# A two-layer graph convolution on one core: in the second layer VectorE evicts the last of a batch's four halves, ScalarE the other three

## The reference

```
def gcn_conv(x, W, b, src, dst, n):
    h = x @ W
    deg = jnp.zeros((n,), h.dtype).at[dst].add(1.0) + 1.0
    dinv = jax.lax.rsqrt(deg)
    norm = dinv[src] * dinv[dst]
    agg = jax.ops.segment_sum(h[src] * norm[:, None], dst, num_segments=n)
    return agg + h * (dinv * dinv)[:, None] + b
h = gcn_conv(emb, W1, b1, src, dst, NTOKEN)     # 64 -> 128 features
nodes = gcn_conv(h, W2, b2, src, dst, NTOKEN)   # 128 -> 64 features
return nodes[input.reshape(-1)].reshape(b_, l_, NINP)
```

## Time and profile before

| | |
|---|---|
| median of 3 runs | 2735.33 us (2734.2 to 2742.24) |
| the profiled execution's own time | 2734.99 us |
| its span in the profile | 2733.2 us |
| second layer, all batches | about 1835 to 2648 us of the span |
| what comes after it (POOL's last DMAs) | about 2648 to 2733 us |
| busy over the span | PE 76%, PEld 63%, DVE 84%, ACT 71%, POOL 34% |

### The profile page before, as it was taken

One profiled execution on the slowest core, in us unless ns is written; L12 is line 12 of the kernel. 1 busy time (PEld: TensorE's weight loads), 2 busy tenths in 40 slices (PEclk: granted clock), 3 DMA queues, 4 the chain that ended last, 5 costly groups with the idle time before them and its releaser, 6 DMA issues.

```text
span 2733.2 us, 87732 instructions
## 1 busy us (share of the span) xinstructions
PE 2070.1 (76%) x36895; PEld 1733.2 (63%) x36895; DVE 2299.6 (84%) x3705; ACT 1928.9 (71%) x5267; POOL 931.5 (34%) x704
## 2 busy tenths in 40 slices
PE   3455555554453599899799999968999999999970
PEld 2344444444321467777678877857888888888860
DVE  9999999999998589888689999956777777777750
ACT  7968898998563796666567777756777677777750
POOL 2000000000000245435736656214223446666656
PEclk8566666666686799999999999989999999999985
DMA  4000000000023334443345656556767764555521
GB/s 113 1 1 1 1 1 1 1 1 1 0 64 49 105 115 134 122 125 109 88 119 135 150 138 151 146 157 180 209 211 214 212 189 141 138 142 144 142 86 18
DMA packets 177449, 277.10 MB, mean 101 GB/s; under 512 B 103578, under 2 KB 116362, under 8 KB 176796
## 3 DMA queue, kind: packets, MB, share of 16 engines
q1 hardware_dynamic: 154748, 244.05, 28.1%
q0 software_dynamic: 22304, 27.40, 8.2%
HBM read 219.68 MB, written 51.81 MB: 99 GB/s over the span
## 4 chain that ended last, share of the span: by engine, by line
PE 42%; DVE 3%; POOL 2%; issue 2%; DMA 1%; SPq 1%; POOLq 0%; ACT 0%; DVEq 0%
PE ps L1328 25%; PE ps L1276 14%; PE ps L1302 1%; POOL out L878 1%; DVE oh L1896 1%; PE ps L1288 1%; DMA arena<-table 1%; SPq L793 1%; POOL arena L869 1%; PE ps L1315 0%; DVE keys L1822 0%; POOL arena L845 0%; DVE ooh L1885 0%; DVE arena L1856 0%; POOL arena L864 0%
## 5 line engine op out<-in xcount | busy, mean ns | idle before, releaser
L1094 ACT ACTIVATE grow_t<-ps 128x384 bf16<-128x384 f32 x2744 | 1144.0, 499 | 528.6 <-PE ps L1276 489.9
L1328 PE MATMUL ps<-grow_t,oh 128*128 128x192 bf16 x10952 | 1053.0, 247 | 5.6 <-issue 5.2
L1328 PEld LDWEIGHTS ps<-grow_t,oh 128*128 128x128 bf16 x10952 | 877.7, 98 | 126.4 <-issue 107.4
L1896 DVE TENSOR_TENSOR oh<-iorep,dl 128x2048 bf16<-128x2048 bf16 x686 | 834.5, 1219 | 118.7 <-PE ps L1328 94.8
L1276 PE MATMUL ps<-arena,keys 128*32 128x192 bf16 x21952 | 608.0, 249 | 61.5 <-DMA arena<-table 20.1
L917 POOL DMA_INDIRECT zring<-table,sidx x296 | 405.4, 1370 | 522.5 <-PE ps L1276 473.3
L1276 PEld LDWEIGHTS ps<-arena,keys 128*32 128x32 bf16 x21952 | 428.6, 97 | 194.0 <-issue 131.3
L825 POOL DMA_INDIRECT arena<-line,row_i x22 | 30.1, 1368 | 860.3 <-DVEq L1645 852.9
L1005 ACT ACTIVATE grow_t<-colf,arena 128x128 bf16<-128x128 f32 x992 | 293.7, 397 | 0.4 <-PE ps L1140 0.4
L1822 DVE TENSOR_SCALAR keys<-keys,rowf 128x2048 bf16<-128x2048 int16 x344 | 258.2, 751 | 40.9 <-DMA keys<-srel 32.5
L1570 DVE TENSOR_TENSOR keys<-keys 128x1280 f32<-128x1280 f32 (+4 forms) x212 | 246.6, 1163 | 9.9 <-ACT keys L1058 6.1
(11 more groups left out here) (246 smaller groups left out, 1923.8 us busy)
## 6 DMA issues: line engine op xcount, KB each, us to landing
keys<-srel SPq DMA_DIRECT2D x344, 512.0 KB
out<-res SPq DMA_DIRECT2D x50, 512.0 KB
table<-arena SPq DMA_DIRECT2D x19, 384.0 KB, 2.8
table<-sgn_l SPq DMA_DIRECT2D x73, 96.0 KB
zring<-table,sidx POOLq DMA_INDIRECT x296
nodes<-arena SPq DMA_DIRECT2D x73, 64.0 KB
arena<-in_L_rec_edge_index SPq DMA_DIRECT2D x2, 1171.5 KB, 5.4
arena<-nodes,oidx POOLq DMA_INDIRECT x108
```

The lines of the kernel that those rows point to most:

```text
L1094: act.activation(grow[:, (layer * NB + j) % DEEP, h * 2 * ROW:(h + 1) * 2 * ROW], psum[HALF_BANK[layer][HB * j + h][0]][:, 0:2 * ROW], ACT ...
L1328: mm = pe.matmul(sums(sl, k), dwin[:, (layer * NB + j) % DEEP, t // TT, k * P:(k + 1) * P, t % TT], grow[:, (layer * NB + j) % DEEP, t * R ...
L1896: dve.tensor_tensor(dwin[:, (layer * NB + j) % DEEP, 0:made[1], :, :], iorep[:, :, :].unsqueeze(1).to_broadcast(made), dl_h[:, j * BT:j * ...
```

## The change

In the second layer, for batches 0 to 341, the fourth half of a batch is copied out of its PSUM bank by DVE instead of ACT, at the very end of DVE's iteration `j+1` (the batch's own number is `j`, so `x = HB * j - 1` in the code). A new semaphore `evac_dve` counts these copies. `by_vector` tells which halves these are, `EVICTED` how many halves ACT has evicted by a given one, and `half_out` has PE wait on the semaphore of the engine that evicts. The last batch's four halves stay with ACT, and the first layer is as it was.

```
+        def by_vector(layer, x):
+            return layer == 1 and x % HB == HB - 1 and x // HB < NB - 1
+        def evicted(layer, x):
+            return (layer * HB * NB + x + 1) - sum(by_vector(layer, y) for y in range(x + 1))
+        EVICTED = [[evicted(layer, x) for x in range(HB * NB)] for layer in range(2)]
...
                         for h in range(HB):
+                            if by_vector(layer, HB * j + h):
+                                continue
                             act.wait_ge(gmm, HB * layer * NB + HB * j + h + 1)
...
+            def half_out(x):
+                if by_vector(layer, x):
+                    pe.wait_ge(evac_dve, x // HB + 1)
+                else:
+                    pe.wait_ge(evac, EVICTED[layer][x] + FREE)
...
                 if what == "half" and n >= 0:
-                    pe.wait_ge(evac, HB * layer * NB + n + 1 + FREE)
+                    half_out(n)
...
                     for h in range(HB):
-                        pe.wait_ge(evac, HB * layer * NB + HB * j + h + 1 + FREE)
+                        half_out(HB * j + h)
...
                         s_build(j // 2 + 1)
+                    if layer and j:
+                        x = HB * j - 1
+                        dve.wait_ge(gmm, HB * NB + x + 1)
+                        dve.tensor_copy(grow[:, (NB + j - 1) % DEEP, 3 * 2 * ROW:4 * 2 * ROW],
+                                        psum[HALF_BANK[1][x][0]][:, 0:2 * ROW]).then_inc(evac_dve, 1)
```

More of the change, by code:

```diff
@@ L346, in gcn_program @@
         evac = sem("evac")
+        evac_dve = sem("evac_dve")
         d_ready = sem("d_ready")
```

## The result

| | before | after |
|---|---|---|
| median of 19 runs each | 2735.78 us (2733.06 to 2742.24) | 2746.7 us (2742.22 to 2753.49) |
| ratio, 95% interval | | 1.0038 [1.0031, 1.0044] |
| span of the profiled execution | 2733.2 us | 2745.9 us |
| DVE busy, ACT busy over the span | 84%, 71% | 89%, 65% |

The changed kernel is 10.9 us slower by the medians, 0.38% by the ratio. That lies in the range (2729 to 2752), but it is just over the 0.3% which the text had called no change: the likeliest case was not the one that came.

What follows compares the result with a forecast made beforehand. The prediction took PE's own stream to bound the second layer. From 2734.99 us, -1 for ACT's waits and +1 to +2 for copies meeting PE's wait gave 2736 us, rounded, range 2729 to 2752.

Steps and rivals of the forecast that it cites:

- the likeliest case: Whole kernel: no change, 2728 to 2743 us, chance 0.77.
- What bounds the kernel, the pace of PE: Second layer: PE's own stream sets the pace, busy 778.15 of 780 us at clock 1.00, 2.32 us a batch.
- The copy's size: Copy on DVE: reports 0.55 to 0.56 us, with the next DVE row 0.46 to 0.48 us behind its start.
- ACT gives up 0.41 us a batch, worth about 1 us: ACT, second layer: three evictions take 1.23 us instead of 1.64; of 5.1 us PE waits, 1 us comes back.
- The room of 0.59 us: DVE, second layer: 199.2 of 780 us free, 0.59 us a batch, of which the copy takes 0.47.
- In time: DVE's iteration: copy done 3.4 us after its start, needed by 4.1 us, so PE's wait is already met.
- +1 to +2 for an occasional batch in which the copy meets PE's wait: Second layer, PE's wait on DVE's copy: costs 1 to 2 us over the whole kernel.
- VectorE becomes the bound: Second layer: a copy over 0.59 us makes DVE the bound; 2746 us at 0.62, 2770 at 0.69; chance 0.14.
- GpSimd is slowed, and the tail grows: POOL's indirect DMAs, slowed by busier DVE, leave ten for the kernel's end, some 12 us: 2747; chance 0.04.
- The sign set for that rival: Kernel's end: a tail after the last scatter over 85 us would speak for GpSimd being slowed.
- The general test: Second layer: prediction wrong if 336 batches take over 788 us.

Runs made afterwards that it cites:

- relief: The kernel before, with ACT leaving the second layer's fourth halves (not the last batch's) unevicted, nobody taking them, PE waiting for the third only; 2721.62 us, ratio 1.0001.
- over: The changed kernel plus a 128x128 fp32 scratch operation on DVE behind each copy, which nothing waits for; 2775.79 us, 1.0148 of the kernel before.
- again: The changed kernel run once more, unaltered, on a chip where the kernel before takes 2720.55 us; 2719.11 us, ratio 0.9995.
- narrow: The changed kernel with DVE's copy taking 4 of the half's 384 columns, the rest not evicted; 2720.94 us, 1.0003 of the kernel before.
- before2: The kernel before, unchanged, run again for its trace and time on a chip of the first kind; 2736.94 us, ratio 1.0003.
- load4: The kernel before plus a 128x384 fp32 maximum on SBUF scratch per second-layer batch on DVE, which nothing waits for; 2722.6 us, ratio 1.0003.

## Why the prediction was right or wrong

- **What bounds the kernel, the pace of PE.** Right. PE is busy 776.31 of 780 us, at a clock of 1.00.
- **The copy's size.** Right: 551 ns against 0.55 to 0.56, the next row 0.46 us later against 0.46 to 0.48.
- **ACT gives up 0.41 us a batch, worth about 1 us.** Right in size: 1.25 us for three halves, ACT 55% busy, and *relief* finds no gain.
- **The room of 0.59 us.** Right, and tested: 0.47 fits, 0.67 costs 0.08 us a batch, where *over* measures 2.40 us for 2.40.
- **In time.** Right: in the changed kernel's stretch there is no row of PE waiting for line 1924.
- **"+1 to +2 for an occasional batch in which the copy meets PE's wait".** This is the step that failed. The copy met no wait; the term should have been about 11 us, and of another kind: 4.3 to 4.7 us of stops in PE's stream and some 6.7 us at the end, which the sum had at 0. Where the changed kernel ran on the other kind of chip, the term is 0 and the sum was right as it stood (*again* 0.9995; *upto*, the change without its last twelve batches, 1.0002). That the range held on the first kind is in part luck: its upper half was there for two rivals, and the loss came by neither.
- **VectorE becomes the bound.** It did not, in the changed kernel. That the loss of 10.9 us is close to this rival's 2746 is chance: its mechanism shows only in *over*.
- **GpSimd is slowed, and the tail grows.** Half of its mechanism is there: POOL's indirect DMAs take 1531 ns instead of 1389, although the copy has one input and that in PSUM. By the Trainium skill, "SBUF — State Buffer", section "Who interferes with whom", it would not hold the shared port. On the other kind of chip the two sizes of copy part clearly (the mean of POOL's L873 is 1391 ns in *narrow* and 1544 in *again*), so the measurement decides against that reading. The other half is missing in the changed kernel: the closing row of requests (from 2645.07 and 2651.26 us on) has 19, 20 and 20 of them in both kernels. POOL's 6.7 us are a wait for the last nodes. In *over* a slower POOL does reach PE, by the 2.59 us for surplus rows, a path that the rival did not name.
- **The sign set for that rival** was badly chosen. A tail of over 85 us was to speak for it, but before already has 2733.2 - 2647.1 = 86.1 us and after 88.9.
- **The general test** ("wrong if 336 batches take over 788 us") did not fire: 335 `dwin` in 780 us is 782 us for 336. The loss lay below its grain and after its stretch.

## What to carry to other kernels

Work out an engine's room from start-to-start distances, not from busy time: here 0.59 us a batch came out to within a hundredth. But use that room up only for a gain, since an engine left with 0.12 us a batch came with a loss of 0.4% on one kind of chip, and no wait names it. Where the view says "remote", look for the event of the semaphore that the instruction waits on: here it was PE's. And measure a change of this size on more than one chip before believing either sign.

## What the runs showed of the hardware

- The same kernel takes 2736 us on one kind of chip and 2720 on another, at the same mean granted clock (0.854 and 0.856). Between the profiles of *before2* and *again* POOL's last DMA moves from 2721.4 to 2702.8 us; 16.2 us of these 18.6 lie ahead of the second layer's first scatter (1855.6 and 1839.4). (*again* is the changed kernel, which costs nothing there.)
- On the first kind of chip the profile can show a matmul ahead of the copy that it reads (2657.02 and 2660.62), and the recorded starts at PE's late end stand 0.7 us apart (2655.60, 2656.32, 2657.02). PE's signal came 21 us behind the last of them, on the other kind of chip 0.26.
- An operation with two fp32 inputs in SBUF slows POOL's indirect DMAs more than the copy out of PSUM. On the other kind of chip the group of surplus rows has a mean of 1296 ns in *narrow*, 1504 ns in *again* and, in *load4*:

```profile
L918 POOL DMA_INDIRECT zring<-table,sidx x139 | 238.1, 1713 | 185.7 <-PE ps L1277 171.4 <-issue 14.3
```
